# Rotated pieces kept in PSUM in the projection stage, and an output stage that works in the product's layout

## The reference

```
h = layernorm(x) * (1 + ca) + sa
a = layernorm(h) * gamma + beta
q, k, v = a @ Wq + bq, a @ Wk + bk, a @ Wv + bv          # 16 heads of 16
q, k = rope(q), rope(k)    # pairs: (x1*cos - x2*sin, x1*sin + x2*cos)
out = softmax(causal(q k' / 4)) v
x = x + ga * (h + out @ Wo + bo)
h = layernorm(x) * (1 + cb) + sb
x = x + gb * mixture_of_experts(h)   # first 2 sequences' tokens, 8 experts, scatter-add
```

## Time and profile before

| | us |
|---|---|
| median of 3 runs (3128.36 to 3128.82) | 3128.5 |
| profiled execution, its own time | 3130.67 |
| its span | 3128.6 |
| PE busy / DVE busy / ACT busy / POOL busy | 2768.8 / 2213.2 / 1818.1 / 1060.7 |
| projection stage, about | 60 to 634 |
| attention stage, about | 634 to 2500 |
| output stage, about | 2502 to 2783 |

### The profile page before, as it was taken

The page is one execution under the profiler, slowest core; times in us unless marked ns, Lnnn a source line. Parts: engine busy times, 40 slices in busy tenths (PEclk is TensorE's granted clock), DMA queues, the critical chain, the costliest instruction groups (busy, mean ns, idle before and its releaser), DMA issues. The chain is left out here.

```text
span 3128.6 us, 48266 instructions
## 1 busy us (share of the span) xinstructions
PE 2768.8 (88%) x17467; PEld 1343.6 (43%) x17467; DVE 2213.2 (71%) x3164; ACT 1818.1 (58%) x3723; POOL 1060.7 (34%) x1294
## 2 busy tenths in 40 slices
PE   1677777669999999999999999999999889957997
PEld 0444444324444444444444444444444267744664
DVE  4999999867777777777777777777777245552221
ACT  1655656507777777777777777777777634421121
POOL 1787778421122111211122112212122166642231
PEclk7899899859999999999999999999999989988999
DMA  3366665663444454444444454445444087752342
GB/s 93 118 195 188 200 200 155 215 132 73 104 92 91 93 104 100 89 89 103 104 90 89 97 104 96 91 90 104 100 92 89 22 286 266 268 189 82 83 115 45
DMA packets 188549, 386.18 MB, mean 123 GB/s; under 512 B 33413, under 2 KB 104485, under 8 KB 175800
## 3 DMA queue, kind: packets, MB, share of 16 engines
q1 hardware_dynamic: 182170, 374.58, 46.7%
q0 software_dynamic: 6144, 8.52, 1.6%
HBM read 240.65 MB, written 144.53 MB: 123 GB/s over the span
## 5 line engine op out<-in xcount | busy, mean ns | idle before, releaser
L922 DVE TENSOR_REDUCE mx<-ps 128x2 f32<-128x1024 f32 (+3 forms) x1216 | 1371.6, 1167 | 397.7 <-PE ps L1010 302.4
L968 ACT ACTIVATE prob<-ps 128x512 f32<-128x512 f32 (+1 forms) x2560 | 1251.7, 560 | 539.8 <-PE ps L1028 531.0
L1003 PE MATMUL ps<-k_rows,q_rows 96*128 96x512 bf16 (+3 forms) x3072 | 910.9, 332 | 47.2 <-DMA k_rows<-k_parts 40.6
L1028 PE MATMUL ps<-q_rows,k_rows 99*128 99x512 bf16 (+3 forms) x3072 | 907.4, 329 | 14.2 <-ACT prob L968 5.8
L861 POOL TENSOR_SCALAR_AFFINE_SELECT prob<-prob 128x512 f32<-128x512 f32 x512 | 318.7, 634 | 1452.9 <-ACT prob L968 1452.9
L1047 PE MATMUL ps<-prob,v_rows 128*32 128x512 f32 (+3 forms) x6144 | 628.8, 497 | 0.0
L1028 PEld LDWEIGHTS ps<-q_rows,k_rows 99*128 99x128 bf16 x3072 | 273.1, 98 | 599.1 <-ACT prob L968 360.0
L1003 PEld LDWEIGHTS ps<-k_rows,q_rows 96*128 96x128 bf16 x3072 | 289.8, 98 | 277.7 <-DVE mx L922 60.8
L1010 PE MATMUL ps<-mask_b,unit_b 128*128 128x128 bf16 (+2 forms) x1408 | 348.6, 248 | 0.0
L666 PE MATMUL ps<-x_t,w_all 128*128 128x512 f32 x512 | 248.5, 631 | 0.0
L1047 PEld LDWEIGHTS ps<-prob,v_rows 128*32 128x32 f32 x6144 | 134.4, 108 | 246.1 <-ACT prob L968 123.3
(11 more groups left out here) (154 smaller groups left out, 2777.6 us busy)
## 6 DMA issues: line engine op xcount, KB each, us to landing
k_rows<-k_parts SPq DMA_DIRECT2D x384, 128.0 KB, 7.3
v_ones<-v_st SPq DMA_DIRECT2D x64, 512.0 KB, 4.3
v_rows<-v_ones SPq DMA_DIRECT2D x64, 512.0 KB, 9.1
att<-o_sb SPq DMA_DIRECT2D x128, 256.0 KB, 2.5
att_b<-att SPq DMA_DIRECT2D x16, 2048.0 KB, 9.9
q_parts<-stage SPq DMA_DIRECT2D x128, 192.0 KB, 3.3
k_parts<-stage SPq DMA_DIRECT2D x128, 192.0 KB, 3.3
q_rows<-q_parts SPq DMA_DIRECT2D x64, 384.0 KB, 4.6
```

What stands on the lines that cost most here:

```text
L922: dve.tensor_reduce(dst, src, AX.X, ALU.max).then_inc(a_free, 1)
L968: nc.scalar.activation(prob[:, (g * NPC + i) % RING, h, 0:w], src, ACT.Exp).then_inc(exp_done, 1)
L1003: ins = pe.matmul(ps[:, at, col:col + w], q[0:ROWS, g, h, i * P:(i + 1) * P], k[0:ROWS, g, h, k0:k0 + w], start=(r == 0), stop=True, skip_ ...
L1028: ins = pe.matmul(ps[:, PS_B + bank(g, n), at:at + w], k[0:AUG, g, h, j * P:(j + 1) * P], q[0:AUG, g, h, q0:q0 + w], start=True, stop=True)
```

## The change

In phase1 `m2` and `qr` are gone from SBUF. The sine products are written over their sources in PSUM, `combine` reads m1 from SBUF and the other operand from PSUM and writes its result over it, and `high` and `take_rest` read PSUM. A pair of banks is therefore held until `take_rest` of its unit; there are now three pairs (six banks), so `project(n)` waits for `take_rest(n-3)` where it waited for `multiply(n-2)`. The transpositions of x have one bank in place of two, and so have the products for v: two tiles share it, half each. No engine reads a bank that another writes at the time, so each half waits for the whole group before it.

```diff
-    PS_X, PS_QK, PS_V = 0, 2, 6
+    PS_X, PS_V, PS_QK, QR = 0, 1, 2, 3
...
+        def half(n, e):
+            return ps[:, PS_QK + n % QR * 2 + 1 - e, :]
+        def turned(n):
+            return ps[:, PS_QK + n % QR * 2:PS_QK + n % QR * 2 + 2, :]
...
-                for m, table in ((m1, cos_t), (m2, sin_t)):
-                    for e in range(2):
-                        c = 2 * which + e
-                        ins = dve.scalar_tensor_tensor(m[:, e, :], ps[:, PS_QK + c, :], bcol[:, c:c + 1], table[:, at],
-                                                       ALU.add, ALU.mult)
+                for e in range(2):
+                    c = 2 * which + e
+                    dve.scalar_tensor_tensor(m1[:, e, :], half(n, e), bcol[:, c:c + 1], cos_t[:, at], ALU.add, ALU.mult)
+                for e in range(2):
+                    c = 2 * which + e
+                    ins = dve.scalar_tensor_tensor(half(n, e), half(n, e), bcol[:, c:c + 1], sin_t[:, at], ALU.add, ALU.mult)
...
-                reuse(dve, rest_done, n - 1)
-                dve.tensor_tensor(qr[:, s, 0, :], m1[:, 0, :], m2[:, 1, :], ALU.subtract)
-                dve.tensor_tensor(qr[:, s, 1, :], m1[:, 1, :], m2[:, 0, :], ALU.add).then_inc(rope_done, 1)
+                dve.tensor_tensor(half(n, 1), m1[:, 0, :], half(n, 1), ALU.subtract)
+                dve.tensor_tensor(half(n, 0), m1[:, 1, :], half(n, 0), ALU.add).then_inc(rope_done, 1)
...
-                dve.tensor_tensor(rest[:, n % 2], qr[:, n % 2], parts(n, 0), ALU.subtract).then_inc(rest_done, 1)
+                dve.tensor_tensor(rest[:, n % 2], turned(n), parts(n, 0), ALU.subtract).then_inc(rest_done, 1)
...
-                nc.scalar.copy(parts(n, 0), qr[:, n % 2]).then_inc(hi_done, 1)
+                nc.scalar.copy(parts(n, 0), turned(n)).then_inc(hi_done, 1)
...
-                reuse(pe, xt_copied, b * T + t - 1)
+                reuse(pe, xt_copied, b * T + first)
...
-                reuse(pe, rope_mul, n - 1)
+                reuse(pe, rest_done, n - QR + 1)
...
-                reuse(pe, v_copied, b * T + t - 1)
+                reuse(pe, v_copied, b * T + t // 2 * 2)
```

```diff
+            def load_den(b):
+                reuse(sp, inv_done, b - 1)
+                sums = att_d[b].rearrange("g (h n) t -> (g h) n t", n=2 * DH)[:, DH, :]
+                sp.dma_start(den[:, b % 2, :], sums.rearrange("h (a c) -> h a c", c=P)).then_inc(den_in[b % 2], DMA)
+            def save_inv(b):
+                sp.wait_ge(inv_done, b + 1)
+                sp.dma_start(rec_d[b].rearrange("h (a c) -> (h a) c", c=P), inv[:, b % 2, :]).then_inc(inv_stored[b % 2], DMA)
+            def load_rec(b):
+                sp.wait_ge(inv_stored[b % 2], (b // 2 + 1) * DMA)
+                reuse(sp, spread, (b - 1) * NQ)
+                sp.dma_start(rec[:, b % 2, :], rec_d[b]).then_inc(rec_in[b % 2], DMA)
...
             for b in range(B):
...
+                if b + 2 < B:
+                    save_inv(b + 2)
+                if b + 3 < B:
+                    load_den(b + 3)
+                    load_x(b + 3)
+                if b + 2 < B:
+                    load_num(b + 2)
+                    load_rec(b + 2)
+                store(b)
+                if b + 2 < B:
+                    load_small(b + 2)
...
+            def invert(b):
+                dve.wait_ge(den_in[b % 2], (b // 2 + 1) * DMA)
+                reuse(dve, inv_stored[b % 2], b // 2 * DMA)
+                dve.reciprocal(inv[:, b % 2, :], den[:, b % 2, :]).then_inc(inv_done, 1)
+            def normalise(b, q):
...
+                dve.wait_ge(spread, b * NQ + q + 1)
+                dve.tensor_tensor(n_t[:, b % 2, k, at], num[:, b % 2, k, at], ps[:, PS_R + q % 2, :], ALU.mult) \
+                   .then_inc(norm_done, 1)
...
+            for b in range(B):
+                if b + 2 < B:
+                    invert(b + 2)
+                if b + 1 < B:
+                    scale_weights(b + 1)
+                for t in range(T):
+                    finish(b, t)
+                    if t % 2 == 1 and b + 1 < B:
+                        normalise(b + 1, t // 2)
...
+            def spread_rec(b, q):
...
+                reuse(pe, norm_done, n - 1)
+                mine = rows[:, k * (HEADS // KC):(k + 1) * (HEADS // KC), :].rearrange("p h n -> p (h n)")
+                pe.matmul(ps[:, PS_R + q % 2, :], mine, rec[:, b % 2, half * HALF:(half + 1) * HALF],
+                          start=True, stop=True).then_inc(spread, 1)
...
+            for b in range(B):
+                for t in range(T):
+                    product(b, t)
+                    if t % 2 == 0 and b + 1 < B:
+                        spread_rec(b + 1, t // 2)
```

More of the change, by code:

```diff
@@ L1113, in phase3 @@
         block = ctx.enter_context(nc.Block())
-        def loop(eng, work):
-            for p in range(2):
-                work(p, 0, p)
-            for it in range(1, B // 2):
-                for p in range(2):
-                    work(it * 2 + p, it, p)
-        def load(sp, b, p):
-            sp.dma_start(gate[:, p], mods_d[b, M_GA, :].partition_broadcast(P)).then_inc(small_in[p], DMA)
-            sp.dma_start(ob[:, p], out_bias_d[b]).then_inc(small_in[p], DMA)
-            sp.dma_start(att[:, p], att_d[b].rearrange("g p t -> p g t")).then_inc(att_in[p], DMA)
@@ new lines, in store @@
+            def store(b):
+                sp.wait_ge(x2_done, b * T + T)
+                dst = sum_d[b * L:(b + 1) * L] if b < SB else out[b]
+                sp.dma_start(dst.rearrange("(t p) d -> p t d", p=P), x2[:, b % 2]).then_inc(stored[b % 2], DMA)
+            load_den(0)
+            load_den(1)
+            load_num(0)
+            load_small(0)
+            save_inv(0)
+            load_x(0)
+            load_rec(0)
+            save_inv(1)
+            load_num(1)
+            load_rec(1)
@@ L1144, in _ @@
+            load_small(1)
+            load_den(2)
+            load_x(1)
+            load_x(2)
             for b in range(B):
-                if b + XR - 1 < B and b >= 1:
-                    load_x(sp, b + XR - 1)
-                store(b, b % 2, sum_d[b * L:(b + 1) * L] if b < SB else out[b])
                 if b + 2 < B:
-                    load(sp, b + 2, b % 2)
+                    save_inv(b + 2)
[8 more added lines that the diff above has]
+                    load_small(b + 2)
@@ L1182, in _ @@
+            for b in range(2):
+                invert(b)
+            scale_weights(0)
+            for q in range(NQ):
+                normalise(0, q)
+            for b in range(B):
[7 more added lines that the diff above has]
+                        normalise(b + 1, t // 2)
         @block.scalar
@@ new lines, in product @@
+            def product(b, t):
+                n = b * T + t
+                if t == 0:
+                    pe.wait_ge(wg_done, b + 1)
+                if t in (0, T // 2):
+                    pe.wait_ge(norm_done, b * NQ + (KC if t == 0 else NQ))
+                reuse(pe, x2_done, n - CR + 1)
+                o = ps[:, PS_C + n % CR, 0:D]
+                pe.matmul(o, ones3[:, :], ob[:, b % 2, :], start=True, stop=False)
+                for k in range(KC):
+                    ins = pe.matmul(o, n_t[:, b % 2, k, t * P:(t + 1) * P], wg[:, b % 2, k, :], start=False,
+                                    stop=(k == KC - 1))
+                ins.then_inc(c_done, 1)
```

174 lines of the change are left out of this document (71 added, 103 removed).

## The result

The changed kernel takes 3111.9 us (median of ten runs, 3092.7 to 3121.9) against 3131.6 (ten runs, 3128.4 to 3134.2). The ratio is 0.9936, with a 95% interval of 0.9916 to 0.9956: some 20 us faster, where 98 were forecast. Its runs spread over 29 us and those of the kernel before over 6; that spread turns out to be part of the answer. The profiled execution took 3102.0 us, 28.7 less than the one before.

The account below looks back on a forecast made before the run. DVE was taken to bound the projection stage and PE the output stage. From the profiled 3130.7 us, gains of 65 and 33 gave 3032.7, less 2.2 for the median 3030 us; range 3000 to 3060.

Parts of the forecast that it names:

- Removed: Projection stage: DVE's wait for POOL in three two-SBUF-operand instructions of each of 64 units goes, gaining 78.6 us.
- what reading and writing PSUM cost: Projection stage: DVE's added access to PSUM, 2.3 us for reading and 3.1 us for writing.
- New waits: Projection stage: waits from fewer transposition banks and busier ACT and PE, charged 0.5 us per batch, 8 us; bounds 0 and 25.
- The rival of slow writes in place: Projection stage: PSUM reads and writes share one way, 136 us in place of 3.1, time 3164; chance 5%.
- chains of ACT and PE: Projection stage: ACT and PE chains of 6.3 us take back most of the gain; half of it gives 3070; chance 10%.
- it now moves 3.64 MB, 10.6 us. No bound: Output stage: DMA per batch falls from 4.49 MB in 13.1 us, to 74% of the time.
- 13.5 us by the same rates: Output stage: inverting, storing and loading the sums behind 2 MB takes 13.5 us, and they are wanted at 14.6.
- The rival of the round trip: Output stage: gate or inverted sums land late, each microsecond costing 16 us; period stays 16.6, time 3064; chance 9%.
- the prediction's own sign of being wrong: Output stage: PE idle for DVE in each batch, or for the load of inverted sums, would show the forecast wrong.
- The start: Output stage: first addition's product at 2519 and first store at 2535, 1 us later than before.
- the term of 14.3 us a period: Output stage: store-to-store period falls from 16.57 to 14.3 us, bounds 12.8 and 16.6; stage gains 33 us.
- that of no change: Both stages: exclusion does not lengthen DVE's three instructions, and the output stage gains nothing; chance 2%.

Follow-up runs that it names:

- num16: Changed kernel with the numerators' rows reordered so that their load's outermost dimension is 16 in place of 8; 3061.9 us, ratio 0.9811.
- fill: Changed kernel plus six unused 128-row products of 512 columns on PE ahead of each wait for the inverted sums; 3104.2 us, ratio 0.9913.
- k128: Changed kernel with the product that spreads the inverted sums contracting over 128 rows, 112 of them zero, in place of 16; 3068.8 us, ratio 0.9794.
- fill16: Changed kernel plus six unused 16-row products of 512 columns on PE ahead of each wait for the inverted sums; 3220.6 us, ratio 1.0299.
- rec_first: Changed kernel with SP issuing the load of the inverted sums before the loads of x and numerators; 3123.1 us, ratio 0.9962.
- best2: Changed kernel with numerators over 16 engines, third gate buffer, gate's load first, inverted sums earlier in SP's order and ahead of x at the start; 3062.3 us.
- p1_only: New projection stage with the output stage of the kernel before; 3058.3 us, ratio 0.9767 against the kernel before.
- the last version: best2 with the spreading product over 128 rows, 112 of them zero; 3038.4 us, ratio 0.9706.
- qr_sbuf: Changed kernel with the combining instructions writing their results to SBUF, so that take_rest reads two SBUF operands again; 3135.3 us, ratio 1.0010.

## Why the prediction was wrong

**The projection stage was right.** Removed: 78.6 us forecast; measured 78, in which what reading and writing PSUM cost in these three lines is already taken off. That cost was forecast at 5.4 us; lines 510 and 511 show 4 and 8 ns over the lone 680 of the earlier trace rows, and line 503 7 ns over the 741 of the earlier trace rows, so under 2 us. The estimate from the Trainium skill, page "VectorE: DVE Perf Modes", section "The TRN2 errata", would have asked 65 ns for each of three instructions: the row decided rightly. New waits: 8 forecast, none found; line 500 waited for PE 6.7 us, and its form waited 9.1 in the trace of before. Not foreseen: the tiny instruction of line 464, 429 ns on the mean before and 1412 now, 16 x 0.98 = 15.7 us. On the other side DVE idled 2.9 us less ahead of line 500 and 1.4 less ahead of line 476, and the tiny line 489 took 1.8 less (696 ns against 809). With 0.5 us for line 503 these make 78 - 0.5 - 15.7 + 2.9 + 1.4 + 1.8 = 68, and the first attention product came 71.1 us earlier:

```profile
576.14 0.59 PE L1009 MATMUL ps<-k_rows,q_rows 96*128 96x128 bf16 x4 [34.61 <-DMA k_rows<-k_parts]
```

Before, it began at 647.20 after 40.58 us of waiting for the same load: 6 us of the 71 are this wait between the stages, which I had taken as unchanged. That leaves 65 for the stage itself, 3 less than the lines add up to. The stage came out at its 65 partly by luck: 8 us charged for waits that never came and some 4 too many for PSUM stand against 16 for an instruction that was not in the sum.

**The rival of slow writes in place** is ruled out: 7 to 13 ns against the 390 at which it would have decided. So is that of the **chains of ACT and PE**, by the 6.7 us of line 500.

**The output stage failed in two steps.** It took 75 us more than forecast: 11 in the start, and 67 in 14 periods of 19.1 us instead of 14.3, less 4 for a shorter last one. The first step is that on DMA: "it now moves 3.64 MB, 10.6 us. No bound". This was bytes over the old rate of 271 GB/s. But a part of the new bytes, the numerators, comes through a transfer with an outermost dimension of 8, and moves at 131 to 160 GB/s. So the next sentence fell too, that the inverted sums take "13.5 us by the same rates" and are wanted at 14.6: their load alone took 10.8 of it, and in six batches they were late, 3.1 us on the mean. `num16` shows this cause by itself: 50 us of the time. DVE's prices, by contrast, held: 422, 679 and 947 ns for the addition, the product and the reciprocal, against 0.43, 0.69 and 0.95 us.

The second step, and the larger in microseconds, is PE's clock, a term that the sum put at nothing without a reason. The forecast took PE's 14 us a batch from the earlier trace rows at full clock and never asked whether the new mix of instructions would keep it; the lower clock cost 47.6 us in 14 periods.

**The rival of the round trip** named the late sums, and the prediction's own sign of being wrong, PE idle for the `rec` load, is what the trace shows. But it mispriced them. It said that each microsecond of lateness is 16 us of time, since PE would wait as long as the sums are late. Measured, 18.5 us of waits behind the start came with 47.6 us by which the lower clock stretched PE's own work. Two things cost clock: pauses, which `num16` reduces and `fill` takes away, and thin products, which `k128` removes at the same pauses (43 us) and `fill16` multiplies (116 us over `fill`, the same columns). A pause alone gives a short fall (`k128`), ten thin products a batch give one without a pause (`fill16`), four don't (`fill`), but they hold the clock down once a pause has let it fall (`rec_first`, `best2`). The spread over runs goes with it: 4 us in `p1_only` and 2 in `fill`, where the clock is steady, and 7 in the last version; 18 in `k128`; 29, 44 and 29 in the kernel after, in `num16` and in `rec_first`. How a run lands in a longer low stretch than another isn't visible in one trace each, and stays open.

**The start** was forecast 1 us longer and is 12.4 longer. The first load of inverted sums was issued only 14.8 us into the stage, at 2446.30, behind 1 MB of x and the numerators, and landed at 2450.37, when the first spreading product began. Four spreading products, 7.16 us at half clock, then stood ahead of the first tile, which began 25.8 us into the stage instead of 15.2. I had named all of this and still put the first tile at 17 us.

**When PE is at full clock and nothing is late**, the term of 14.3 us a period was right: 14.4 to 15.0 in seven periods of the kernel after, 14.0 in `best2`, 13.8 in the last version. The mean fell short of it, as that state held in half of the batches.

**The range** was narrower than its own chances. The prediction says that less than 2 in 10 lie outside 3000 to 3060, but the rival of slow writes (3164), that of the round trip (3064), that of no change and most of the second one lie outside, together more than 20 in 100.

## What to carry to other kernels

Price a DMA by its outermost dimension too, not by its bytes alone: reordering rows so that it is 16 rather than 8 took the DMA engines' share from 0.53 to 0.99 here and was worth 50 us. When a change puts thin matmuls (few rows) into PE's stream, try padding them with zero rows: here the columns were the same, the time no longer, and the clock came back sooner after a pause. Run the two halves of a change apart before keeping both: the projection stage alone was 54 us faster than the whole change. And when a wait is taken away and the time doesn't follow (`rec_first`), look at PE's clock and at the wait behind it before doubting the mechanism.

## What the runs showed of the hardware

The granted clock of TensorE fell from 2.4 to 1.2 GHz (1.00 to 0.50 in the rows) without any pause, while PE ran 7.74 us of products that contract over 16 rows (`fill16`), and it stayed at 1.2 GHz for whole batches (26.18 us in `rec_first`) with PE busy all the time, four such products among the wide ones of each batch. With 128 rows, zeros for the most part, it was back 8 us after a pause (`k128`). The Trainium skill, page "TensorE: Matmul & The Clock Gate", section "HAM oscillation — how this bites in real kernels", puts such falls down to PE waiting for DMAs between groups of products. By that, covering each wait should have been enough: `fill` agrees (1.00 throughout), `fill16` doesn't (0.61 to 0.79), and the measurement decides.

A tiny VectorE instruction, 8 elements from two tensors in SBUF, took 1.41 us on the mean in the kernel after, where it fell beside a 2.13 us one of POOL, and 190 ns in `qr_sbuf`. Whoever frees the large instructions from that exclusion can hand it on to a small one.
